# Eight row blocks of one expert moved from the expert stage to the end of a graph network's second layer

## The chip, the core and the metric

The kernel runs on one core of one Trainium2 chip. The metric is the device time of one execution in microseconds (us). The core has five engines that run their own instruction streams and meet through semaphores: PE (matrix multiply, with PEld for its weight loads), DVE (vector), ACT (scalar), POOL (GpSimd) and SP (which here only starts transfers). Transfers are started by SP, ACT and POOL and carried by 16 DMA engines.

## What is computed

A two-layer graph convolution over 3125 nodes with 256 features and 50000 edges, followed by a mixture of 16 experts in which each node uses its two best. The part after the first layer norm, cut to what matters here:

```python
for W, b, g, be in ((W1, b1, ln_g1, ln_b1), (W2, b2, ln_g2, ln_b2)):
    h_res = h
    h = _gcn_conv(h, row, col, ew, dis, W, b)
    h = jax.nn.relu(_layernorm(h, g, be)) + h_res
x = x + h
...
xn = _layernorm(x, axis=-1)
gate_logits = xn @ gate_w + gate_b
topk_vals, topk_idx = jax.lax.top_k(gate_logits, 2)
topk_w = jax.nn.softmax(topk_vals, axis=-1)
h = jax.nn.relu(jnp.einsum('bsh,ehf->bsef', xn, w1) + b1)
expert_out = jnp.einsum('bsef,efh->bseh', h, w2) + b2
y = xn + sum over the two choices of topk_w * expert_out
x = x + _layernorm(y) * gamma + beta
```

## The kernel before

`program` runs three stages in turn, each a block of five engine streams: `gnn` (both graph layers and the choice of experts), `experts` (the expert networks) and `combine` (the weighted sum, the last layer norm and the output). All engines meet at a barrier between two stages.

**The graph layers.** Nodes stand in 25 tiles of 128. A layer is a product of a weighted adjacency with a table of the transformed nodes: PE sums 25 matmuls for each of 26 groups of cells (L1373), which the code calls a turn; DVE and ACT split the sum into three bf16 parts (`take_rest`, `take_low`, L818 and L824), PE folds them onto node tiles (`combine(k)`, L1265), and DVE with ACT finishes a tile (`finish_tile`, L829 to L866): bias, layer norm, relu, residual, and in layer two also the norm that the experts read. Layer two works from the last tile to the first; `r` counts its tiles, so r = 24 is the last finished.

**The choice of experts**, in layer two, two turns behind the tile: PE turns the normalised rows (`turn_x2`, L1306) and multiplies by the gate (`gate`, L1314), DVE takes the two best experts (`choose`, L873 to L891), PE counts how many nodes chose each expert before (`count`, L1321), and DVE computes each node's slot in its expert's region (`seat`, L897 to L902). POOL keeps the residual (`keep_x1`, L566) and scatters node numbers and target rows to the slots in DRAM (L577, two transfers per tile), here called the homes.

**The experts.** Rows are worked in blocks of 128 slots of one expert. For a block, SP loads the 128 node numbers and targets (`load_ids`, L1512), POOL gathers the rows (`fetch`, L1468), PE turns them (`turn_x`, L1542), ACT copies them out of PSUM (L1634), PE multiplies by w1 (`up`, L1559), DVE adds b1 and applies relu (`relu_h`, L1709), PE multiplies by w2 (`down`, L1571), DVE adds row and b2 (L1719, L1724), and POOL scatters the 128 results (`send`, L1474). PE's stream is written as up of block b+1, turn of block b+2, down of block b. The first `FIXED` = 4 blocks are the first blocks of experts 0 to 3; the rest come from a table that DVE computes behind the barrier (L1680 to L1699, from the counts of all nodes), with a copy of the block's w1 by ACT into `w1s` (L1628). 58 blocks are worked always, and up to 6 more only where a register says that the table has more (`more`).

**The weights.** w1 and w2 of all experts lie in the memory that the graph layers use before. SP loads them as that memory comes free: most of w2 between the turns, w1 behind the last turns (L149, L154), and the four last halves (`UPS_LATE`, `DOWNS_LATE`) in the expert stage after ten loads of node numbers.

```python
for b in range(IDS_FIRST):
    load_ids(b)
for e in UPS_LATE:
    load_up(sp, e)
for e in DOWNS_LATE:
    load_down(sp, e)
```

## Time and profile before

| what | value |
|---|---|
| median of 3 runs | 1191.6 us (1189.5 to 1194.8) |
| the profiled execution: its own time | 1186.33 us |
| its span, first to last instruction | 1184.6 us |
| mean granted clock of PE | 0.976 of full speed |
| busy in the span: PE, DVE, ACT, POOL | 91%, 60%, 33%, 51% |
| row blocks worked in the expert stage | 58 |

The page gives busy shares over the whole span, and a row of the span in 40 slices for each engine, the granted clock of PE (PEclk) and the transfers. Shares over the span hide the places where PE stands still, so the stage between the second layer and the steady part of the expert stage is read from the timelines, instruction by instruction, and from windows cut at its borders.

### The profile page before, as it was taken

To read this page: it belongs to the slowest core of one execution; us is meant where nothing else is said; L and a number is where in the kernel's file an instruction comes from. 1 tells how busy PE (TensorE), PEld (TensorE's weight loads), DVE (VectorE), ACT (ScalarE), POOL (GpSimd) and SP (SyncE) were. 2 spreads that over 40 slices of the span, in tenths; PEclk is the share of its full clock that TensorE was granted. 3 is DMA by queue.
4 is the path that set the end of the run, shared out by engine and by line. 5 is a ranking of instruction groups with operands and counts; after the bars stand their busy time and mean duration, and the time that the engine had idled before them with its cause. 6 is when DMAs were issued, how large, how long until landed. Compare 5 with 4: busy or idle time off the path is not lost. (4 is left out here: it accounts for less than half of the span.)

```text
span 1184.6 us, 19696 instructions
## 1 busy us (share of the span) xinstructions
PE 1074.9 (91%) x6393; PEld 932.6 (79%) x6396; DVE 716.2 (60%) x2173; ACT 395.2 (33%) x908; POOL 605.6 (51%) x659
## 2 busy tenths in 40 slices
PE   3787889999999999799998999999991999999966
PEld 2666768888888888688787788888871899999965
DVE  8999990144454444234477777777776455555537
ACT  4758675212222222112222122222221233333347
POOL 6777777777777777760012121121123455555526
PEclk9999999999999999899999999999995999999989
DMA  6999920334333413131365345445436522222237
GB/s 239 312 392 378 373 114 2 118 112 144 135 112 127 152 57 112 56 112 56 128 241 187 129 163 182 160 149 193 165 125 210 179 72 70 71 73 73 72 94 264
DMA packets 80164, 180.80 MB, mean 153 GB/s; under 512 B 29042, under 2 KB 58364, under 8 KB 74044
## 3 DMA queue, kind: packets, MB, share of 16 engines
q1 hardware_dynamic: 48792, 151.67, 35.4%
q0 software_dynamic: 19776, 15.76, 4.9%
q10 hardware_dynamic: 11492, 12.07, 3.1%
q8 instruction: 54, 0.88, 0.3%
q14 instruction: 50, 0.41, 0.1%
HBM read 122.12 MB, written 57.33 MB: 151 GB/s over the span
## 5 line engine op out<-in xcount | busy, mean ns | idle before, releaser
L507 POOL DMA_INDIRECT weights_by_cell<-w_cell,cell x391 | 390.4, 999 | 131.6 <-issue 121.7
L1373 PE MATMUL ps<-x_rows,w 128*128 128x256 f32 x1250 | 283.5, 381 | 8.0 <-DMA w<-weights_by_cell 8.0
L1373 PE MATMUL ps<-w 128*128 128x256 f32 x1164 | 267.9, 382 | 0.0
L1373 PEld LDWEIGHTS ps<-x_rows,w 128*128 128x128 f32 x1250 | 234.7, 191 | 39.2 <-DMA w<-weights_by_cell 8.8
L1373 PEld LDWEIGHTS ps<-w 128*128 128x128 f32 x1164 | 213.9, 190 | 25.5
L566 POOL TENSOR_TENSOR x_rows<-hot,beta_b 128x256 f32<-128x256 f32 x25 | 18.1, 724 | 287.6 <-DVE hot L857 287.6
L1709 DVE TENSOR_SCALAR hidt<-ps,b1t 128x128 f32<-128x128 f32 x232 | 66.0, 344 | 89.3 <-PE ps L1559 88.5
L1559 PEld LDWEIGHTS ps<-xt,w1s 128*128 128x128 f32 x880 | 106.8, 192 | 5.0 <-ACT w1s L1628 2.2
L1571 PE MATMUL ps<-w,hidt 128*128 (+1 forms) x464 | 109.8, 379 | 0.0
L1559 PE MATMUL ps<-xt,w1s 128*128 128x128 f32 x880 | 107.2, 275 | 1.8 <-ACT xt L1634 1.8
L1474 POOL DMA_INDIRECT expert_rows_by_token<-yb,ids x58 | 57.5, 992 | 92.9 <-DVE yb L1724 92.5
L1571 PEld LDWEIGHTS ps<-w,hidt 128*128 128x128 f32 x464 | 83.6, 190 | 9.0
L1123 PE MATMUL ps<-key_part,pick 128*128 128x256 f16 x196 | 59.2, 408 | 33.1 <-DVE layer L714 32.4
L818 DVE TENSOR_TENSOR layer<-ps,layer 128x256 f32<-128x256 f32 x52 | 22.1, 426 | 86.1 <-ACT layer L1035 85.3
L1468 POOL DMA_INDIRECT xb<-normalised_rows,ids x60 | 59.0, 983 | 26.6 <-PE ps L1542 16.3
L1634 ACT ACTIVATE xt<-ps 128x256 f32<-128x256 f32 x60 | 23.0, 384 | 140.6 <-PE ps L1542 140.6
L1265 PE MATMUL ps<-layer 128*128 128x256 bf16 x444 | 56.9, 272 | 9.1 <-issue 7.1
L1159 PE MATMUL ps<-w,hot 128*128 128x75 bf16 x400 | 64.6, 319 | 0.0
L1628 ACT ACTIVATE w1s<-w 128x1024 f32 x56 | 59.2, 1057 | 7.5 <-DMA w<-in_L_ffn_w_dram 5.3
L1265 PEld LDWEIGHTS ps<-layer 128*128 128x128 bf16 x444 | 41.8, 98 | 24.8 <-issue 16.9
L577 POOL DMA_INDIRECT token_and_home_of_slot<-pair,slot_id x50 | 50.2, 1005 | 14.2 <-issue 11.3
L838 DVE COPY_PREDICATED layer<-mark,zeros 128x256 f32<-128x256 int32 x50 | 22.5, 450 | 55.3 <-ACT mark L1043 54.5
(250 smaller groups left out, 1554.8 us busy)
## 6 DMA issues: line engine op xcount, KB each, us to landing
w<-weights_by_cell SPq DMA_DIRECT2D x46, 1600.0 KB, 6.9
weights_by_cell<-w SPq DMA_DIRECT2D x26, 1600.0 KB, 8.7
w<-in_L_ffn_w_dram SPq DMA_DIRECT2D x32, 512.0 KB, 9.3
weights_by_cell<-w_cell,cell POOLq DMA_INDIRECT x391
w<-in_x_dram ACTq DMA_DIRECT2D x1, 3072.0 KB
hot<-in_x_dram ACTq DMA_DIRECT2D x24, 128.0 KB, 7.6
normalised_rows<-hot ACTq DMA_DIRECT2D x24, 128.0 KB, 6.5
out_dram<-w SPq DMA_DIRECT2D x24, 128.0 KB
```

What stands on the lines that cost most here:

```text
L507: pool.indirect_dma_start(adj[:, :], bass.IndirectOffsetOnAxis(ap=cell[0:m, c:c + 1].bitcast(U32), axis=0), w_cell[0:m, n, half * CH + j:h ...
L577: pool.indirect_dma_start(home[:, :], bass.IndirectOffsetOnAxis(ap=slot_id[0:m, k, d:d + 1].bitcast(U32), axis=0), pair[0:m, k, d, :], Non ...
L1123: mm = pe.matmul(bank(at, k * SBE, (k + 1) * SBE), pick[:, j:j + 1].to_broadcast([P, P]), key_part[:, g, :], start=True, stop=True)
L1159: mm = pe.matmul(bank(6, 0, 3 * NT), hot[:, i % DRING, :, k], hot_w[:, i % DRING, :, :, k].rearrange("p a b -> p (a b)"), start=(i == 0 an ...
L1265: mm = pe.matmul(bank(2 + i % 3, 0, D), fold_bits[:, k % 2, cols], ov_parts[:, k % 2, c, :], start=begins and c == 0, stop=ends and c == P ...
L1373: mm = pe.matmul(ov_bank(k), ring[:, place_of(k), s * P:(s + 1) * P], tab[q][:, s, :], start=(s == 0), stop=(s == NT - 1))
L1468: pool.indirect_dma_start(xb[:, b % ring, :], None, x2_dram[0:N, :], bass.IndirectOffsetOnAxis(ap=ids[:, b % IDS, 0:1].bitcast(U32), axis= ...
L1474: pool.indirect_dma_start(planes[:, :], bass.IndirectOffsetOnAxis(ap=ids[:, b % IDS, 1:2].bitcast(U32), axis=0), yb[:, b % 2, :], None).th ...
L1559: mm = pe.matmul(ph[s][:, f * P:(f + 1) * P], w, xt[:, s, c, :], start=(c == 0), stop=(c == KD - 1))
L1571: mm = pe.matmul(py[s], hidt[:, s, c, :], w, start=(c == 0), stop=(c == KF - 1))
L1628: act.activation(w1s[:, k, :, :].rearrange("p c f -> p (c f)"), w1[:, bass.ds(e * (KD * F), KD * F)], ACT.Copy).then_inc(w1_ready, 1)
L1709: ins = dve.tensor_scalar(hidt[:, s, c, :], ph[s][:, c * P:(c + 1) * P], bias, 0.0, ALU.add, ALU.max)
```

## The change

Before layer two ends, the counts over its first 19 tiles (r = 0 to 18) give the expert most chosen so far; experts 5, 6 and 12 are excluded, because their w2 comes late. Up to eight full blocks of that expert are known by then. `popular` on DVE picks it and writes the eight block places, SP loads its w1, b1 and b2 into buffers of their own (`w1e`, `b1e`, `b2e`), POOL gathers the rows, and the blocks are worked by PE, ACT and POOL: blocks 0 to 3 inside `gnn` between the last instructions of layer two (the down of block 3 behind the barrier), blocks 4 to 7 at the head of `experts`. For blocks 0 to 5 ACT does the relu and takes the output from PSUM, and POOL adds row and bias; from block 6 (`BY_ACT`) on DVE does both as before. The later stage works 50 blocks always (`RARE` is 14), the table leaves out what was taken (`taken`), and the four last weight halves are loaded before the barrier. Several buffers are shared or moved to make room (`key_part`, `cell`, `w_cell`, `mark`, `vec`, `wmat`, `own_diag`, `over`).

```diff
-IDS = 12
+EARLY, EARLY_IN, BY_ACT, EARLY_T = 8, 4, 6, 19
+IDS = 8
-RARE = 6
+RARE = 6 + EARLY
+GATE_AT = 6
...
+        def early_fetch(pool, j):
+            if j >= RING:
+                pool.wait_ge(x_turned, j - RING + 1)
+                pool.wait_ge(y_ready, j - RING + 1)
+            pool.wait_ge(ids_in[j % IDS], 16 * (j // IDS + 1))
+            pool.indirect_dma_start(
+                xb[:, j % RING, :], None, x2_dram[0:EARLY_T * P, :],
...
+        def early_bias(pool, j):
+            pool.wait_ge(x_turned, j + 1)
+            pool.wait_ge(xb_in[j % RING], 16 * (j // RING + 1))
+            pool.tensor_tensor(xb[:, j % RING, :], xb[:, j % RING, :], b2e, ALU.add).then_inc(x_biased, 1)
+
+        def early_add(pool, j):
+            pool.wait_ge(y_taken, j + 1)
+            pool.wait_ge(x_biased, j + 1)
+            pool.tensor_tensor(yb[:, j % 2, :], yb[:, j % 2, :], xb[:, j % RING, :], ALU.add).then_inc(y_ready, 1)
...
+        def early_relu(act, j, ph):
+            act.wait_ge(h_ps, j + 1)
+            if j >= 2:
+                act.wait_ge(out_ps, j - 1)
+            for c in range(KF):
+                ins = act.activation(hidt[:, j % 2, c, :], ph[:, c * P:(c + 1) * P], ACT.Relu, bias=b1e[:, c:c + 1])
+            ins.then_inc(hidt_ready, 1)
```

In `gnn`, SP's stream behind the last load of layer two:

```diff
+                for k in range(EXPERTS // WGROUP):
+                    sp.wait_ge(w_in[k], 16 * sum(e // WGROUP == k for e in DOWNS_IN_LAYER))
+                sp.sem_inc(early_w, 1)
+                sp.wait_ge(early_ready, 1)
+                sp.wait_ge(tab_ready[1], NT)
...
+                sp.wait_ge(homes_first, 32 * EARLY_T)
+                for j in range(EARLY):
...
+                    sp.dma_start(ids[:, j % IDS, :], home[bass.ds(at * P, P), :]).then_inc(ids_in[j % IDS], 16)
+                    if j == 2:
+                        sp.dma_start(b1e[:, :], eb1[bass.ds(expert, 1), :].rearrange("a (c p) -> p (a c)", p=P),
+                                     allow_slow_non_contiguous=True).then_inc(early_w, 16)
+                        sp.dma_start(b2e, eb2[bass.ds(expert, 1), :].to_broadcast([P, D])).then_inc(early_w, 16)
                 sp.wait_ge(ov_ps, 2 * VT - 2)
                 for e in (3, 4):
                     load_up(sp, e)
...
                 for e in UPS_IN_TIME:
                     load_up(sp, e)
+                sp.wait_ge(fold_ready, 2 * VT)
+                load_down(sp, DOWN_LATE)
+                sp.wait_ge(agg_read, 2 * NT)
+                load_up(sp, UP_LAST)
+                sp.wait_ge(z_ready, 2 * NT)
+                for e in DOWNS_LAST:
+                    load_down(sp, e)
```

In `gnn`, DVE in `seat`, then ACT:

```diff
+                    if r == EARLY_T:
+                        popular()
+                    if r == EARLY_T + 1:
+                        take_popular()
...
                 def marks(q, d, i):
+                    last = i == 2 * NT - 1
+                    if last:
+                        early_xt(act, 1, early_px)
+                        act.wait_ge(early_w, 49)
+                        early_relu(act, 0, bank(2))
                     act.wait_ge(y_made, i + 1)
...
+                    if last:
+                        early_relu(act, 1, bank(1))
                     act.wait_ge(z_made, i + 1)
...
+                    if last:
+                        early_y(act, 0, early_py)
+                        early_xt(act, 2, early_px)
```

In `gnn`, PE behind the last turn:

```diff
+                pe.wait_ge(early_w, 49)
...
+                turn_rows(pe, 0, early_px)
                 turn_x2(NT - 2)
+                pe.wait_ge(xt_ready, 1)
+                turn_rows(pe, 1, early_px)
+                pe.wait_ge(agg_read, 2 * NT - 1)
+                early_up(pe, 0, bank(2))
                 combine(2 * VT - 1)
                 gate(NT - 2)
                 count(NT - 3)
+                early_up(pe, 1, bank(1))
+                early_down(pe, 0, early_py, place)
+                turn_rows(pe, 2, early_px)
+                early_up(pe, 2, bank(2))
+                early_down(pe, 1, early_py, place)
                 turn_x2(NT - 1)
+                turn_rows(pe, 3, early_px)
                 gate(NT - 1)
                 count(NT - 2)
+                pe.wait_ge(agg_read, 2 * NT)
+                early_up(pe, 3, bank(3))
                 count(NT - 1)
...
+                early_down(pe, 2, early_py, place)
```

In `experts`, POOL's stream behind the barrier:

```diff
+                    fetch(6)
+                    finish_early(2)
+                    fetch(7)
+                    early_bias(pool, 4)
+                    finish_early(3)
+                    early_bias(pool, 5)
                     for k in range(XRING):
                         pool.wait_ge(x2_out[k], 16 * -(-(NT - k) // XRING))
...
+                    fetch(8)
+                    finish_early(4)
+                    fetch(9)
+                    finish_early(5)
+                    fetch(10)
```

`early_xt`, `early_up`, `early_down`, `early_y`, `turn_rows` and `send_rows` do for an early block what `copy_x`, `up`, `down`, the output addition, `turn_x` and `send` do for a later one; `popular` is a chain of small operations on 16 or 8 values, shown as rows below.

How the order of instructions moves, at three places. **PE, from the last turn's end to the barrier.** Before, only the turn of the last tile's rows (L1306), its gate (L1314), the counts (L1321, L1322) and the fold (L1265) stand there:

```order
L1306 MATMUL ps<-ident,hot 128x128 x2
L1265 MATMUL ps<-layer 128x256 x3
L1314 MATMUL ps<-gwt,ht 128x16 x2
L1321 MATMUL ps<-both,below 128x16
L1322 MATMUL ps<-before,ones 128x16
```

After, the same instructions (now L1521, L1480, L1529, L1538, L1539) have early work between them; a piece from the down of block 0 (its last weights) on:

```order
L231 MATMUL ps<-ident,xb 128x128 x2
L238 MATMUL ps<-xt_e,w1e 128x128 x8
L249 MATMUL ps<-w,hidt 128x256 x4
L1521 MATMUL ps<-ident,hot 128x128 x2
L231 MATMUL ps<-ident,xb 128x128 x2
L1529 MATMUL ps<-gwt,ht 128x16 x2
L1538 MATMUL ps<-both,below 128x16
L1539 MATMUL ps<-before,ones 128x16
L238 MATMUL ps<-xt_e,w1e 128x128 x8
```

L231 is the turn of an early block, L238 its up, L249 its down: the up of block 2 and the down of block 1 now stand ahead of the turn of the last tile's rows.

**POOL, the last homes.** Before, the last residual and the homes of the last three tiles (L577, two each) stand directly ahead of the barrier:

```order
L566 TENSOR_TENSOR x_rows<-hot,beta_b 128x256
L577 DMA token_and_home_of_slot<-pair,slot_id 59392x2 x6
L357 UNCONDITIONAL_BRANCH
L1453 UNCONDITIONAL_BRANCH
L1455 IOTA bnum 128x60
```

After (L716 the residual, L723 the homes, L195 and L200 the early additions, L204 an early block's results):

```order
L188 DMA xb<-normalised_rows,ids 128x256 x3
L195 TENSOR_TENSOR xb<-xb,zeros 128x256 x2
L723 DMA token_and_home_of_slot<-pair,slot_id 60416x2 x2
L200 TENSOR_TENSOR yb<-yb,xb 128x256
L204 DMA expert_rows_by_token<-yb,ids 66816x256
L716 TENSOR_TENSOR x_rows<-hot,beta_b 128x256
L195 TENSOR_TENSOR xb<-xb,zeros 128x256
L200 TENSOR_TENSOR yb<-yb,xb 128x256
L204 DMA expert_rows_by_token<-yb,ids 66816x256
L723 DMA token_and_home_of_slot<-pair,slot_id 60416x2 x4
L195 TENSOR_TENSOR xb<-xb,zeros 128x256
```

The homes of the last two tiles now stand behind the addition and the sending of early block 1.

**DVE, in `finish_tile` of tile r = 21**, ahead of the seat of tile 19 (L1096), new:

```order
L1068 TENSOR_TENSOR early_score<-ps,may_early 128x16
L1069 MAX early_top<-early_score 128x8
L1070 TENSOR_SCALAR fixed_one<-eids 128x16
L1071 MAX_INDEX early_at<-early_top,early_score 128x8
L1072 TENSOR_SCALAR early_f<-early_at 128x1
L1073 CAST early_e<-early_f 128x1
L1074 TENSOR_SCALAR early_place<-early_f 128x1
L1075 TENSOR_SCALAR early_lead<-early_f 128x1
L1076 SCALAR_TENSOR_TENSOR early_rows<-early_lead,early_top 128x1
L1077 TENSOR_SCALAR early_has<-rows_to,early_rows 128x8
L1078 SCALAR_TENSOR_TENSOR early_e<-early_f,early_place 128x1
L1079 TENSOR_REDUCE early_n<-early_has 128x1
```

Three more of the kind follow, and two in the next tile (`take_popular`); nothing is taken out of DVE's stream there.

## Rows read from the trace of the kernel before

**Rows 1.** Windows: stretch, busy us (count) PE PEld DVE ACT POOL, PEclk, DMA share, GB/s.

```profile
800.00:885.40 85.40, 85.11 (x451) 72.88 (x449) 66.13 (x222) 18.50 (x47) 16.80 (x19) 1.00 0.47 160
885.40:888.80 3.40, 0.59 (x5) 0.35 (x5) 2.66 (x12) 1.19 (x4) 2.00 (x3) 1.00 0.56 193
888.80:918.00 29.20, 4.68 (x25) 3.35 (x24) 18.97 (x68) 4.10 (x9) 10.79 (x14) 0.50 0.63 208
918.00:924.00 6.00, 6.00 (x34) 6.00 (x33) 1.13 (x4) 0.38 (x1) 1.93 (x2) 0.57 0.76 250
936.00:1139.00 203.00, 203.00 (x1420) 191.86 (x1419) 103.25 (x328) 78.12 (x109) 104.42 (x106) 1.00 0.23 70
```

**Rows 2.** PE's timeline, end of layer two to the first blocks: start, us.

```profile
884.82 0.59 PE L1373 MATMUL ps<-w 128*128 128x256 f32 x2
...
888.66 0.52 PE L1265 MATMUL ps<-layer 128*128 128x256 bf16 x3 [1.89 <-DVE layer L824]
...
897.49 0.69 PE L1306 MATMUL ps<-ident,hot 128*128 128x128 f32 x2 [7.59 <-DVE hot L866]
...
903.92 0.20 PE L1385 MATMUL ps<-before,ones 128*128 128x16 bf16 x1 [0.99 <-DVE slot_id L902]
...
918.10 6.13 PE L1559 MATMUL ps<-xt,w 128*128 128x128 f32 x32
924.07 0.38 PE L1542 MATMUL ps<-ident,xb 128*128 128x128 f32 x2
924.29 1.89 PE L1571 MATMUL ps<-w,hidt 128*128 128x256 f32 x8
```

**Rows 3.** PE's timeline, the steady part and the last block's down.

```profile
935.47 2.02 PE L1559 MATMUL ps<-xt,w1s 128*128 128x128 f32 x16 [1.82 <-ACT xt L1634]
...
943.01 1.95 PE L1559 MATMUL ps<-xt,w1s 128*128 128x128 f32 x16
944.79 0.38 PE L1542 MATMUL ps<-ident,xb 128*128 128x128 f32 x2
945.01 1.89 PE L1571 MATMUL ps<-w,hidt 128*128 x8
...
1139.06 1.89 PE L1571 MATMUL ps<-w,hidt 128*128 x8
```

**Rows 4.** SP's timeline in the expert stage: node numbers, then the late weight halves.

```profile
909.05 10.40 SPq L1512 DMA_DIRECT2D ids<-token_and_home_of_slot  x10
919.50 0.51 SPq L149 DMA_DIRECT2D w<-in_L_ffn_w_dram  x1
920.06 3.56 SPq L154 DMA_DIRECT2D w<-in_L_ffn_w_dram  x3
```

**Rows 5.** DVE's timeline: one turn's chain, then the last tile's seat.

```profile
876.03 0.42 DVE L824 TENSOR_TENSOR layer<-layer 128x256 bf16<-128x256 f32 x1 [0.26 <-ACT layer L1037]
...
888.09 0.42 DVE L824 TENSOR_TENSOR layer<-layer 128x256 bf16<-128x256 f32 x1 [0.26 <-ACT layer L1037]
...
900.18 0.17 DVE L897 TENSOR_TENSOR rank<-ps,base 128x16 f32<-128x16 f32 x1 [1.14 <-PE ps L1322]
...
901.03 0.17 DVE L873 TENSOR_TENSOR logit<-ps,gbias 128x16 f32<-128x16 f32 x1
...
903.69 0.17 DVE L902 CAST slot_id<-which 128x2 int32<-128x2 f32 x1
...
904.87 0.19 DVE L1678 TENSOR_TENSOR gap<-best 128x25 f32<-128x25 f32 x1
```

**Rows 6.** POOL's timeline: last residual, last home, first gather.

```profile
895.86 0.72 POOL L566 TENSOR_TENSOR x_rows<-hot,beta_b 128x256 f32<-128x256 f32 x1 [8.00 <-DVE hot L857]
...
905.42 0.97 POOL L577 DMA_INDIRECT token_and_home_of_slot<-pair,slot_id  x1 [0.30 <-issue]
...
911.59 1.00 POOL L1468 DMA_INDIRECT xb<-normalised_rows,ids  x1 [4.84 <-DMA ids<-token_and_home_of_slot]
```

**Rows 7.** Issues from 904 to 925: KB each, median us from issue to landing.

```profile
w<-in_L_ffn_w_dram SPq DMA_DIRECT2D x4, 512.0 KB, 10.2
...
xb<-normalised_rows,ids POOLq DMA_INDIRECT x6, 5.0
```

**Rows 8.** POOL's groups by shape: count | busy us, mean ns | idle before.

```profile
L566 POOL TENSOR_TENSOR x_rows<-hot,beta_b 128x256 f32<-128x256 f32 x25 | 18.1, 724 | 287.6 <-DVE hot L857 287.6
L1837 POOL TENSOR_TENSOR w<-w,x_rows 128x256 f32<-128x256 f32 x25 | 18.0, 726 | 19.9 <-ACT w L1831 18.4
```

**Rows 9.** Issues from 885 to 905, as in rows 7.

```profile
w<-in_L_ffn_w_dram SPq DMA_DIRECT2D x10, 512.0 KB, 9.5
...
token_and_home_of_slot<-pair,slot_id POOLq DMA_INDIRECT x7, 5.5
b1r<-in_L_ffn_b_dram ACTq DMA_DIRECT2D x1, 24.0 KB, 2.3
```

More of the change, by code:

```diff
@@ new lines, in early_y, with turn_rows @@
+        def early_y(act, j, py):
+            act.wait_ge(out_ps, j + 1)
+            if j >= 2:
+                act.wait_ge(y_out[j % 2], 16 * (j // 2))
+            act.activation(yb[:, j % 2, :], py, ACT.Copy).then_inc(y_taken, 1)
+        def turn_rows(pe, j, px):
+            pe.wait_ge(xb_in[j % RING], 16 * (j // RING + 1))
+            for c in range(KD):
+                mm = pe.transpose(px[:, c * P:(c + 1) * P], xb[:, j % RING, c * P:(c + 1) * P], ident[:, :])
+            mm.then_inc(x_turned, 1)
@@ L1320, in count @@
                         pe.wait_ge(rank_read, r)
+                    if r == EARLY_T:
+                        pe.matmul(bank(5, EXPERTS, 2 * EXPERTS), ones[:, :], before[:, r % 2, :], start=True, stop=True)
                     pe.matmul(bank(5, 0, EXPERTS), below[:, :], both[:, r % 2, :], start=True, stop=False)
@@ L1603, in _ @@
                     with pe.If(more(pe, "pe")):
[L1604 to L1605 removed]
+                        for b in range(USUAL, ALL):
+                            block_of_rows(b)
                 def load_b2(act, lo, hi, landed):
```

499 lines of the change are left out of this document (331 added, 168 removed).

## The prediction

> **What bounds the kernel now.** I read the page's slices first, then windows cut at the borders of the stages, then the timelines of PE, DVE, POOL and SP between the second layer and the steady expert stage. The windows [rows 1] show PE full in both neighbours: 85.1 of 85.4 us in layer two's last turns, and all of the 203 us from 936 to 1139. Between 885.4 and 918 it works 5.3 of 32.6 us, and from 888.8 on at half the granted clock (0.50, the 1.2 GHz level; 1.00 elsewhere). So the gap between two PE-bound stages is what early work can fill. What ends it is a chain of other engines [rows 2, 5, 6]: last sum at 885.4, last tile finished by DVE (its rows turned at 897.5), two more rounds of gate, choice and count, last seat at 903.9, last home issued from 905.4 to 906.4, node numbers fetched from 909.05 [rows 4], first gather at 911.6 [rows 6], first up at 918.1, and the even rhythm from the down at 924.29 on [rows 2].
>
> That rhythm sets the price of a block. The first down starts at 924.29, the 58th and last at 1139.06 [rows 2, 3]: 57 periods in 214.77 us, less one stall. The stall is the 1.82 us ahead of the up at 935.47 [rows 3]; it is put down to ACT's copy, which itself waited for the last four weight halves, issued from 919.50 to 923.62 [rows 4] and 10.2 us in landing [rows 7]. (214.77 - 1.82) / 57 = **3.736 us a block**.
>
> **What is removed.** The stage behind the even rhythm's start has eight blocks fewer: 8 x 3.736 = **29.9 us**. The four weight halves now go out behind the other ten before the barrier, some 20 us earlier, and land before the first wait for all weights; the stall goes: **1.8 us**. Nothing takes its place there, since ACT's copies of w1 then run two blocks ahead. Together 31.7 us; this is spent again, in part, in three places.
>
> **1. DVE's chain through layer two.** `popular` has 15 instructions and `take_popular` 2, all on 16 values or fewer. Four such linked ones take 901.03 - 900.18 = 0.85 us [rows 5], 0.21 each: 17 give 3.6. Five of them have nothing waiting for their result directly, which brings it down to some 2.9. I take **3.4**. Is there cover? One turn's DVE chain runs from L824 at 876.03 to L824 at 888.09 [rows 5]: 12.06 us, and the fold of the last turn on PE waits for it (1.89 us, DVE L824, rows 2), after the sums have ended. So the loop DVE, fold, DVE is what ends layer two; what is added to it arrives at its end in full.
>
> **2. PE, ACT and POOL inside the last tile.** ACT and PE work in order, so each early instruction stands in front of something. Walked with the durations of the rows: up 0 ends some 0.7 us after the last fold could start. Up 2 and down 1 stand ahead of the turn of the last tile's rows, which DVE waits for: up 2 waits for ACT's copy of the turned rows, this for the output of block 0, and both end about 2 us after the rows are ready. The relus by ACT, four of at most 0.4 us, fall into its waits for DVE (4.1 us of work in 29.2, rows 1). The first delay is partly taken up by DVE's wait for PE's next count (1.14 us at 900.18, rows 5). I take **1.8**, between 0 (all in the gaps) and 4.5 (both delays plus one more hand-over). POOL then has, between the last-but-two homes and the last, an addition, a sending and another residual: 23 us of work from the residual of tile 23 on, done at about the time when the last seat comes, so it adds nothing more; what is behind it, if it were late, is SP's wait for the homes.
>
> Of the DMAs, each engine issues its own: eight node number loads, w1, b1, b2 by SP (at 857 to 867, when SP waits for sums), six gathers by POOL before the barrier. They land long before PE asks, at about 889. The weights on SP's queue are 14 halves in a row instead of ten (9.5 us each in landing, rows 9); the last sends and homes share the DMA engines with them.
>
> **3. Behind the barrier.** Before: 924.3 - 904.8 = 19.5 us to the first steady down (DVE's first instruction there is at 904.87, rows 5). After: six ups, seven turns and five downs stand before the same point, at 1.78, 0.22 and 1.73 us [rows 3]: 20.9. ACT's two starts of transfers and its first copy stand ahead of the first up, 1.4, and the transpose of b1 is 0.4: 22.7. On POOL the gather of block 8 stands behind two gathers, two sends (1.3 each with the gap), four additions (0.9 each with the gap) and three iotas: some 9.3, begun 2 us after the barrier, when POOL still issues homes; with 5.0 us to landing [rows 7] its rows are there 16.3 us after the barrier, where PE would want them after 14.8. PE waits 1.6: 24.3, that is **4.8** more than before. Ends: 2.5 (steady PE work alone, with the copies hidden) and 7.5 (both gathers 6 to 7 as the homes were, and DVE's table, begun at its iotas, later too). I take 4.8 because its three parts have rows at this place. The node numbers for block 8 come by then: homes 5.5 [rows 9] after an issue that ends 2 us behind the barrier, and 2 for the load, 9.5 against POOL's 11.3.
>
> By the Trainium skill, page "SBUF — State Buffer", section "Who interferes with whom", GpSimd and VectorE share a port pair: a vector instruction with two SBUF inputs contends with a GpSimd instruction that reads SBUF. POOL's 128x256 addition takes 724 ns beside layer two and 726 ns in the last stage [rows 8], so no row shows it stretched. By that rule up to four additions before the barrier would wait for a 0.43 us instruction each, 1.7 us by estimate, and the gain would be 20 instead of 21.7; I go by the rows.
>
> **Sum.** 31.7 - 3.4 - 1.8 - 4.8 = **21.7 us**. From the profiled execution's 1186.3 that is 1164.6. This execution lies 5.3 below the median of the three runs; from the median, 1191.6 - 21.7 = **1169.9**, stated as 1170. With all three losses at their good ends (2.9, 0, 2.5) it is 1165.3, with all at their bad ones (3.6, 4.5, 7.5) 1175.5.
>
> **The rivals.** *The clock stays at half.* PE fell to 0.50 from 888.8 to 918 with 16% of that stretch worked, and two ups then took 6.13 us at 0.57 where one takes 1.95 at 1.00 [rows 1 to 3], so 1.1 more for an up and, in proportion, 1.0 for a down. Ups 0 to 2 and downs 0 and 1 in part (some 3.5) and the first three pieces behind the barrier (3.2) would cost about 7: 1177. Against it: PE's gaps from 889 on are 1 to 3 us by my walk, and a 1.82 us gap at 933.6 left the clock at 1.00. By the Trainium skill, page "TensorE: Matmul & The Clock Gate", section "What's actually happening", the throttled state is the default and activity releases it; the trace agrees (0.57, then 1.00, once blocks run).
>
> *POOL or the transfers hold block 8.* If gathers land after 6 to 7 us and the sends of blocks 0 and 1 come as late, POOL's line of waits (an addition waits for ACT, ACT for the down, the next gather for the addition) grows by 5 to 9 us: 1175 to 1179. For it: POOL has no slack by my walk. Against: the rhythm of one gather and one send a block was kept from 936 on.
>
> *Slower: the early weights come late.* PE waits for w1e, b1e and b2e ahead of the turn of tile 23's rows, and all that ends layer two is queued behind that wait on PE. b1e is 512 single words; the nearest row is the b1 load of 24 KB, 2.3 us [rows 9], and no row shows such single words. Needed at about 889, they would cost a microsecond for each after that; the gain is gone when they land at 911, and at 925 the time is 1206. Against: SP can start them at 857.
>
> *It doesn't do what it says.* If the chosen expert had fewer than eight full blocks, spare blocks would be worked and the table would pass its limit of 46; 14 more blocks would follow (52 us): about 1222. The reference's routing for these inputs gives expert 2 with 1527 rows in the first 19 tiles, against 1152 needed, and 46 later blocks, exactly the limit; so this is nearly excluded.
>
> **Chances.** Forecast 0.63 (1163 to 1175), half clock 0.15, POOL or transfers 0.11, these two together, no more than 0.5% from no change, 0.05; weights late 0.05 and too few blocks 0.01, both slower. 0.5%, 6 us, is about what a measurement of this kernel can tell from no change. Faster 0.89, same 0.05, slower 0.06. The range, 1163 to 1181, takes in the bounds of the sum, the runs' spread of 2 to 3 us below and the two milder rivals; it leaves out some 0.15 to 0.2.
>
> **What would show it.** Right: 8 x 3.74 us fewer in the steady stage, no wait ahead of the first copied w1, the last fold on PE some 3 to 4 us later than 888.7, the last home 5 to 6 later than 905.4, the down of block 8 at about 934, and the granted clock at 1.00 through the gap. Wrong: the clock at 0.50 behind 889, PE waiting for block 6's, 7's or 8's rows by more than 2 us each, a wait of PE for w1e, or a rhythm other than 3.74.

## The result and the profile after

| | before | after | ratio, 95% interval |
|---|---|---|---|
| median of 4 runs each | 1192.18 us | 1177.24 us (1175.62 to 1182.97) | 0.9891 [0.9863, 0.9919] |
| the changed kernel run again: 6 runs, against 17 of before | 1190.81 us | 1177.90 us | 0.9896 [0.9878, 0.9915] |

The change is faster, by 14.9 us in the first comparison and 12.9 in the second. The forecast was 1170, a gain of 21.7, so 7 to 9 us of it are missing. The profiled execution took 1175.62 us with a span of 1173.9.

PE's timeline shows the core of the change as it was forecast. These are rows of the changed kernel from the last fold to the steady stage (start, us), answering to [rows 2, 3]:

```profile
896.31 0.49 PE L1480 MATMUL ps<-layer 128*128 128x256 bf16 x3
...
898.92 1.89 PE L249 MATMUL ps<-w,hidt 128*128 x8
900.64 0.38 PE L231 MATMUL ps<-ident,xb 128*128 128x128 f32 x2
903.58 2.94 PE L238 MATMUL ps<-xt_e,w1e 128*128 128x128 f32 x16 [2.55 <-ACT xt_e L212]
906.31 2.71 PE L249 MATMUL ps<-w,hidt 128*128 x8
908.85 0.38 PE L1521 MATMUL ps<-ident,hot 128*128 128x128 f32 x2
...
938.88 1.89 PE L1805 MATMUL ps<-w,hidt 128*128 128x256 f32 x8
...
948.07 1.95 PE L1792 MATMUL ps<-xt_e,w1s 128*128 128x128 f32 x16
...
1121.73 1.89 PE L1805 MATMUL ps<-w,hidt 128*128 x8
```

L238 and L249 are ups and downs of early blocks, L1521 is the turn of the last tile's rows. The first steady down, block 8's, starts at 938.88 and the last one at 1121.73: 49 periods of 3.732 us. The up on the first copied w1, at 948.07, has no wait ahead of it: the 1.82 us stall of [rows 3] is gone. Behind the barrier PE is nearly never idle, as the windows show (columns as in [rows 1]):

```profile
889.00:900.00 11.00, 10.30 (x72) 9.33 (x71) 8.56 (x32) 4.16 (x13) 6.24 (x7) 1.00 0.51 179
900.00:910.00 10.00, 7.14 (x36) 6.05 (x35) 6.80 (x20) 4.57 (x16) 6.89 (x9) 0.83 1.05 349
910.00:918.00 8.00, 5.63 (x40) 4.58 (x40) 4.93 (x22) 1.89 (x7) 6.33 (x11) 1.00 1.04 356
918.00:936.00 18.00, 17.99 (x124) 16.45 (x123) 14.29 (x31) 5.37 (x17) 15.08 (x17) 1.00 0.51 108
936.00:1121.70 185.70, 185.70 (x1297) 175.47 (x1296) 94.07 (x301) 71.07 (x99) 97.41 (x99) 1.00 0.27 80
```

Where PE worked 4.68 of 29.2 us at a granted clock of 0.50 [rows 1], it now works 23.07 of 29 at 1.00, but for the stretch from 900 to 910 (0.83). To see where the missing microseconds are, I cut every profile of this study at the same five instructions: A, from the start to DVE's statistics of tile 17 of layer two (still ahead of the changed region); B, from there to the rank of the last tile; C, from there to the first steady down; D, to the start of the last matmul of the last down; E, to the end of POOL's last addition; F, to the end of the span.

| us | A | B | C | D | E | F |
|---|---|---|---|---|---|---|
| before | 804.8 | 98.3 | 21.3 | 216.3 | 40.1 | 4.0 |
| after | 808.7 | 104.5 | 25.6 | 184.4 | 41.3 | 9.3 |
| e1_again (the changed kernel) | 809.9 | 103.3 | 25.3 | 184.4 | 41.6 | 9.3 |
| e2_pe_pad | 813.3 | 104.5 | 25.3 | 184.4 | 43.3 | 9.3 |
| e3_weights_only (of before) | 805.2 | 98.3 | 22.2 | 214.2 | 39.9 | 4.0 |
| e4_pick_twice | 813.0 | 107.4 | 26.3 | 184.4 | 44.0 | 9.3 |
| e5_no_drain | 808.1 | 104.4 | 26.3 | 184.4 | 42.1 | 4.6 |
| e6_pool_pad | 811.8 | 104.5 | 25.7 | 184.4 | 41.2 | 9.3 |
| e7_before_no_drain (of before) | 809.6 | 98.3 | 20.6 | 217.6 | 40.3 | 4.1 |
| e8_small_adds | 811.0 | 102.5 | 26.5 | 184.4 | 42.6 | 9.3 |
| e9_more_gathers | 807.9 | 104.4 | 25.4 | 184.4 | 47.7 | 4.5 |
| e10_act_order | 810.6 | 102.9 | 26.2 | 184.4 | 44.3 | 4.6 |
| e11_pick_beside | 812.8 | 100.1 | 25.3 | 184.4 | 41.5 | 4.6 |
| e12_before_gathers (of before) | 810.9 | 98.2 | 20.5 | 217.2 | 44.6 | 3.9 |

Three things stand out. A varies from profile to profile of one and the same program, mostly with PE's waits for the adjacency; from tile 0 of layer two to tile 17 all fourteen profiles take 214.1 or 214.2 us, so the spread lies ahead of layer two. So the difference of two spans says little here, and what an experiment does is read from its own stage. B is 103.3 in e1 and 104.4 to 104.5 in the other profiles of the changed kernel with the same code there; the section on the choice of the expert shows why. And F, a stage that the change doesn't touch, is 5.3 us longer in every profile of the changed kernel that keeps its closing barrier, except e9. SP's waits at the end, in the changed kernel:

```profile
SPq L2055 <- PEq L2055: 5.0, 1, 5.0
SPq L2055 <- DMA out_dram<-w: 3.8, 1, 3.8
```

and before:

```profile
SPq L1786 <- DMA out_dram<-w: 3.3, 1, 3.3
SPq L1786 <- PEq L1786: 0.2, 1, 0.2
```

After the last store has landed SP waits another 5.0 us in the closing barrier, where it waited 0.2.

### The profile page after: what moved, and what is told of

It reads as the page before. It is cut to its first block and busy times, and to the rows that moved or that the text cites. A ratio compares the mean times of both kernels' runs of the same rounds, so it can differ in the third digit from the quotient of the medians.

```text
span 1173.9 us, 19637 instructions
## 1 busy us (share of the span) xinstructions
PE 1076.2 (92%) x6397; PEld 932.1 (79%) x6397; DVE 713.3 (61%) x2156; ACT 395.7 (34%) x930; POOL 617.2 (53%) x676
## 5 line engine op out<-in xcount | busy, mean ns | idle before, releaser
L650 POOL DMA_INDIRECT weights_by_cell<-hidt x391 | 392.0, 1003 | 132.5 <-issue 123.0
L1590 PEld LDWEIGHTS ps<-w 128*128 128x128 f32 x1164 | 214.6, 191 | 25.7
L716 POOL TENSOR_TENSOR x_rows<-hot,beta_b 128x256 f32<-128x256 f32 x25 | 18.1, 723 | 279.3 <-DVE hot L1030 279.3
L204 POOL DMA_INDIRECT expert_rows_by_token<-yb,ids x58 | 57.6, 994 | 78.0 <-DVE yb L1990 75.5
L1967 DVE TENSOR_SCALAR hidt<-ps,b1t 128x128 f32<-128x128 f32 x200 | 56.3, 344 | 67.4 <-PE ps L1792 67.4
L1805 PE MATMUL ps<-w,hidt 128*128 (+1 forms) x400 | 94.6, 379 | 0.0
L1792 PEld LDWEIGHTS ps<-xt_e,w1s 128*128 128x128 f32 x752 | 91.4, 192 | 2.4
L1792 PE MATMUL ps<-xt_e,w1s 128*128 128x128 f32 x752 | 91.5, 275 | 0.0
L1338 PE MATMUL ps<-xt_e,pick 128*128 128x256 f16 x196 | 58.9, 406 | 34.7 <-DVE layer L887 34.2
L1805 PEld LDWEIGHTS ps<-w,hidt 128*128 128x128 f32 x400 | 72.1, 190 | 7.7
L1480 PE MATMUL ps<-layer 128*128 128x256 bf16 x444 | 57.6, 274 | 8.3 <-issue 8.2
L1480 PEld LDWEIGHTS ps<-layer 128*128 128x128 bf16 x444 | 42.0, 98 | 24.1 <-issue 15.9
L1880 ACT ACTIVATE xt_e<-ps 128x256 f32<-128x256 f32 x52 | 20.0, 384 | 117.1 <-PE ps L231 117.1
L723 POOL DMA_INDIRECT token_and_home_of_slot<-pair,slot_id x50 | 50.2, 1004 | 11.9 <-issue 11.1
L1011 DVE COPY_PREDICATED layer<-mark_a,zeros 128x256 f32<-128x256 int32 x50 | 22.5, 450 | 55.7 <-ACT mark_a L1251 54.9
L1338 PEld LDWEIGHTS ps<-xt_e,pick 128*128 128x128 f16 x196 | 16.5, 117 | 49.0 <-DVE layer L887 39.0
```

Of the source, the lines that this page charges most:

```text
L204: pool.indirect_dma_start(planes[:, :], bass.IndirectOffsetOnAxis(ap=ids[:, j % IDS, 1:2].bitcast(U32), axis=0), yb[:, j % 2, :], None).th ...
L650: pool.indirect_dma_start(adj[:, :], bass.IndirectOffsetOnAxis(ap=cell[0:m, c:c + 1].bitcast(U32), axis=0), w_cell[0:m, n, half * CH + j:h ...
L723: pool.indirect_dma_start(home[:, :], bass.IndirectOffsetOnAxis(ap=slot_id[0:m, k, d:d + 1].bitcast(U32), axis=0), pair[0:m, k, d, :], Non ...
L1011: link(dve.copy_predicated(y, mark_a[:, 0:D].bitcast(I32), zeros[:, 0:D]))
L1338: mm = pe.matmul(bank(at, k * SBE, (k + 1) * SBE), pick[:, j:j + 1].to_broadcast([P, P]), key_part[:, g, :], start=True, stop=True)
L1480: mm = pe.matmul(bank(2 + i % 3, 0, D), fold_bits[:, k % 2, cols], ov_parts[:, k % 2, c, :], start=begins and c == 0, stop=ends and c == P ...
```

## The experiments

### The changed kernel again, and PE's code moved

e1_again is the changed kernel without an edit. e2_pe_pad puts waits on PE ahead of the last stage:

```diff
         def _(pe):
+            for k in range(128):
+                pe.wait_ge(diag_ready, 1)
             for t in range(NT):
```

> The changed kernel as it is, with a second profiled execution. In the first, 7 of the 21.7 us that were forecast are missing, and the trace shows differences outside the changed region: +3.9 us in the graph stage (1.4 in the first 15 us, 2.2 at a wait for the adjacency at 496) and 5.0 us at the very end, where SP waits for PE's queue after the last store has landed. Theory (the end belongs to the new program, the graph stage is chance): the 5.0 us at the end come again, within 0.5; the +3.9 us do not, the second profile has them at 0 to 2; median 1177, plus or minus 2. Rival (all of it chance, the terms of the gap were too small): the wait at the end is under 1 us here, and the losses between the two layers and block 8 come out above 11 us.

> The changed kernel with 128 waits on a semaphore that is long set, put on PE ahead of its first product of the last stage, where PE waits 9 us for the first rows anyway. It changes nothing but the place of PE's later instructions in its code. Theory (PE's queue is late at the end since its last instructions fall behind a border of its code that has to be loaded): the 5.0 us wait of SP for PE's queue at the end is under 1 us, the time 4 to 5 us under the changed kernel, about 1172.5. Rival (something else holds PE's queue there, such as the length of the program or the last products): the wait stays at 5.0 us and the time at 1177.

e1_again: 1177.90 us; the wait at the end is 5.0 us again, so it is the program's own. A is 809.9, 5.1 above the first profile of before: the +3.9 did not go away, against my theory. But three more profiles of programs that are the old one up to there (e3, e7, e12) have 805.2, 809.6 and 810.9, and the ten of the changed program lie between 807.9 and 813.3. The means are 3 us apart, the spread within either is as large: whether the change costs something in the graph stage stays open.

e2_pe_pad: ratio 0.9919 [0.9900, 0.9938], 1181.48 us, and the wait is 5.0 us as before. The 128 waits were not free: the first product of the last stage comes 13.8 us behind the end of the last down instead of 9.2. The theory on PE's code has fallen all the same, since the wait did not move. The name in that row misled me: all engines count up one semaphore in the barrier, and the row names one that does so. The rows of the barrier's line itself (its instructions by engine: duration in ns, min/median/max, first and last start) name the late one. Of the changed kernel:

```profile
L2055 PEldq DRAIN  x1: 957/957/957, 1160.1 to 1160.1; - x1
...
L2055 POOLq DRAIN  x1: 10411/10411/10411, 1163.2 to 1163.2; - x1
```

and of the one before:

```profile
L1786 POOLq DRAIN  x1: 2732/2732/2732, 1179.3 to 1179.3; - x1
```

PE's queue had ended its own DRAIN there at 1161. POOL's DRAIN lasts until 1163.2 + 10.4 = 1173.6, and the span ends at 1173.9.

### The closing DRAIN

e5_no_drain leaves POOL's DRAIN out of that barrier, e7_before_no_drain does so in the kernel before; SP still waits for all stores:

```diff
-    with nc.Block() as block:
+    with nc.Block(no_gpsimd_drain=True) as block:
```

e6_pool_pad puts 64 waits on POOL, as e2 did on PE:

```diff
         def _(pool):
+            for k in range(64):
+                pool.wait_ge(diag_ready, 1)
             for t in range(NT):
```

> The changed kernel, with POOL's DRAIN in the closing barrier of the last stage left out; SP's wait for the landing of all stores stays. In every profile of the changed program so far POOL's DRAIN there takes 10.41 us, in those of the program before 2.73, and SP waits 5.0 and 0.2 us after the stores have landed. Theory (the DRAIN is what SP waits for, the name PE in that row is only the engine that arrived at the same semaphore): 5.0 us less, 1172.9 against 1177.9, and the span ends 0.3 us after the last store has landed. Rival (PE's queue is late on its own): 1177.9 and the wait of 5.0 us stays.

> The changed kernel with 64 waits on a long-set semaphore on POOL ahead of its first addition of the last stage, where POOL has 18 us of idle time. Theory (the DRAIN is long since the instruction behind it lies across a border of POOL's code and has to be loaded): the DRAIN falls from 10.4 to some 3 us, the time by 5 to 1173. Rival (it is the work that POOL itself has to close, the same in each run): DRAIN 10.4 and 1178 again.

> The kernel before with the same DRAIN left out. Theory: there it is hidden behind the landing of the stores but for 0.2 us, so the time stays at 1190.8, within 1. Rival: it delays more than the trace shows, 1188 or less.

e5: 1172.10 us against 1192.42 of before in the same comparison, ratio 0.9835 [0.9813, 0.9858]. F falls from 9.3 to 4.6 us, and SP's rows of that kernel read as they did before the change:

```profile
SPq L2055 <- DMA out_dram<-w: 3.8, 1, 3.8
SPq L2055 <- PEq L2055: 0.2, 1, 0.2
```

So the DRAIN is what held the end, and it cost some 5 us of the gain. With it gone the gain is 20.3 us by medians. e7: ratio 0.9995 [0.9982, 1.0009]: in the program before, the DRAIN was hidden behind the stores. e6: 0.9894 [0.9871, 0.9917], and DRAIN again 10.41 us: moving POOL's code by 64 waits does not change it.

What makes it long? e9 adds four gathers to the changed kernel, behind POOL's last send:

```diff
+                    for k in range(4):
+                        pool.indirect_dma_start(
+                            xb[:, k, :], None, x2_dram[0:NT * P, :],
+                            bass.IndirectOffsetOnAxis(ap=ids[:, 0, 0:1].bitcast(U32), axis=0)).then_inc(y_out[0], 16)
+                    pool.wait_ge(y_out[0], 16 * (USUAL // 2) + 64)
                     pool.wait_ge(table_ready, 1)
```

> The changed kernel with four more gathers of 128 rows by POOL, behind its last send and awaited there, in the idle time ahead of the last stage; DRAIN kept. All that is asked is the length of POOL's DRAIN, 10.41 us in five profiles of the changed program, 2.73 in two of the one before, 64 more waits without effect. Theory (it depends on how many indirect transfers POOL has issued, or on what is left of them in its queue): another length than 10.41, by 0.2 us or more. Rival (it depends on something else in the program): 10.41 again. The time is for neither, a few us above 1178.

```profile
L2060 POOLq DRAIN  x1: 2897/2897/2897, 1168.5 to 1168.5; - x1
```

e9: 1176.04 us in one run, with E 6 us longer, since the last stage starts behind the four gathers, and DRAIN 2.90 us. So the four transfers change the DRAIN, where 64 more waits did not. e12_before_gathers adds the same four to the kernel before:

```diff
+                    for k in range(4):
+                        pool.indirect_dma_start(
+                            xb[:, k, :], None, x2_dram[0:N, :],
...
+                    pool.wait_ge(y_out[0], 16 * (usual // 2) + 64)
```

> The kernel before with the same four more gathers by POOL behind its last send, DRAIN kept. In the changed kernel they brought POOL's DRAIN from 10.41 to 2.90 us. Theory (the length goes up and down with how many indirect transfers POOL has issued, 559 in both programs without the four): another length than 2.73 here, possibly the long one. Rival (the short DRAIN is what such gathers leave behind, or what the program before has anyway): 2.7 to 2.9 again.

There the DRAIN goes from 2.73 to 3.06 us (one run, 1197.08 us). In both programs the length moves when POOL issues more, but the number of transfers does not set it: both programs issue 559 indirect ones, with 2.73 us in the one and 10.41 in the other. What does set it stays open.

### The late weights alone

e3_weights_only moves only SP's last four loads in the kernel before:

```diff
+                sp.wait_ge(fold_ready, 2 * VT)
+                load_down(sp, 12)
+                sp.wait_ge(agg_read, 2 * NT)
+                load_up(sp, 5)
+                sp.wait_ge(z_ready, 2 * NT)
+                for e in (5, 6):
+                    load_down(sp, e)
...
-                    for e in UPS_LATE:
-                        load_up(sp, e)
-                    for e in DOWNS_LATE:
-                        load_down(sp, e)
```

> The kernel before with only the last four weight halves moved: they go out behind the other ten in the graph stage. Theory (the prediction's second term): PE's 1.82 us wait ahead of the first copied weights is gone and nothing takes its place: 1192.2 - 1.8 = 1190.4, no block saved. Rival: the halves now share the DMA engines with the last homes and the first gathers, the first up comes later by as much as was won: 1192, and the gap to the down at 924.3 is longer by 1 to 2 us.

Ratio 0.9999 [0.9986, 1.0011]. D is 2.1 us shorter, so the stall is gone; C is 0.9 longer than in the profile of before. PE's timeline of e3 shows both:

```profile
910.61 0.37 PE L1537 MATMUL ps<-ident,b1r 64*128 64x64 f32 x1 [6.14 <-DMA b1r<-in_L_ffn_b_dram]
...
925.58 1.89 PE L1574 MATMUL ps<-w,hidt 128*128 128x256 f32 x8
...
934.78 1.95 PE L1562 MATMUL ps<-xt,w1s 128*128 128x128 f32 x16
```

No wait stands at 934.78, but b1, which [rows 9] has landing in 2.3 us, is waited for here for 6.14 us, while it was 4.8 before. Theory and rival are both right in part, and the time can't tell them: by itself this edit buys at most 1.7 us (the lower end of the interval). The stall and the start of the blocks go together: in the two later profiles of the old code, e7 and e12, the stall is 3.09 and 2.73 us instead of 1.82, and C is 0.7 and 0.8 shorter, so that C and D together are 237.6, 238.2 and 237.7 us in the three, and 236.4 in e3. D also gives the cleanest price of the blocks: 214.2 - 184.4 = 29.8 us for eight, both without the stall.

### The choice of the expert

e4_pick_twice runs the 15 instructions of the choice two times:

```diff
                     if r == EARLY_T:
+                        popular(False)
                         popular()
```

> The changed kernel with the 15 instructions that choose the expert done twice, one pass after the other, at the same place on DVE. Theory (the loop of DVE and PE has no slack in layer two, so the chain arrives in full at the end): 2.4 us more by the traced length of the chain to 3.1 by the prediction's 0.21 us an instruction: 1179.6 to 1180.3. Rival 1 (it is partly covered, the loss seen there is a short drop of PE's clock): under 1 us more. Rival 2 (the longer pause drops PE's clock for longer): over 4 us more.

Ratio 0.9933 [0.9910, 0.9956], 1182.92 us, 5.0 over e1. By the time alone rival 2 would have it (over 4), but both intervals reach 2 us or more to either side, and A and E, which the edit doesn't touch, are 3.1 and 2.4 longer in its profile than in e1's. B is 107.4, 2.9 to 4.1 us over the two profiles of the changed kernel. To tell chain and clock apart I cut B at DVE's statistics of single tiles (tile 17 to 20 takes 38.0 us in every profile):

| us | tile 20 to 21 | 21 to 23 | 23 to 24 | 24 to the last rank | granted clock, 21 to 22 |
|---|---|---|---|---|---|
| before | 12.7 | 24.9 | 11.2 | 11.6 | 1.00 |
| after | 15.1 | 26.2 | 11.2 | 14.1 | 0.87 |
| e1_again | 15.1 | 25.0 | 11.2 | 14.1 | 1.00 |
| e4_pick_twice | 17.6 | 26.5 | 11.1 | 14.1 | 0.75 |
| e8_small_adds | 15.1 | 26.2 | 11.1 | 12.1 | 0.87 |
| e10_act_order | 15.1 | 26.2 | 11.1 | 12.5 | 0.88 |
| e11_pick_beside | 12.7 | 25.2 | 11.2 | 13.1 | 1.00 |

The choice stands in the first of these stretches: it costs 2.4 us there, and the second pass of e4 2.5 more. So the chain arrives in full, and the theory holds for it. The second stretch shows the drop of PE's clock that the rivals speak of: 1.3 us more behind the choice in the first profile, 0.1 in e1. PE waits equally long in both, ahead of the turn (0.67 us) and of the fold, and runs the fold at two speeds (the first row is of the first profile, the second of e1):

```profile
870.08 1.80 PE L1480 MATMUL ps<-layer 128*128 128x256 bf16 x9 [1.41 <-issue]
...
871.25 1.14 PE L1480 MATMUL ps<-layer 128*128 128x256 bf16 x9 [1.41 <-issue]
```

The granted clock is 0.66 from 870 to 875 in the first profile and 1.00 from 871 to 876 in e1. e2, e5, e6 and e9 are like the first (26.0 to 26.2 us, 0.87 to 0.88). So PE pauses for the choice, and where the clock falls behind that pause it costs up to 1.3 us more; in e4 the clock is 0.50 from 875 to 880, and the stretch is 1.6 longer than before the change. So the rivals are right that the clock takes part, but with the smaller share.

e11_pick_beside (which also has e10's order and no DRAIN) takes these 17 instructions out of their row: a list hands one out behind each of the main chain's instructions.

```diff
+                def beside():
+                    if side:
+                        make, linked = side.pop(0)
+                        if side_at[0]:
+                            dve.wait_ge(v, side_at[0])
+                        ins = make()
...
                 def link(ins):
-                    dve.wait_ge(v, did(ins))
+                    at = did(ins)
+                    beside()
+                    dve.wait_ge(v, at)
```

> The kernel with ACT's order changed and without the DRAIN, and the 17 instructions that choose and note the expert no longer in a row: each is issued behind one of the main chain's instructions, ahead of that one's wait. Theory (term 1 is latency, not work): 2.5 to 3 us of the 3.4 come back, the last seat at 99.5 to 100.5 behind the start of tile 17, the time 2.5 to 3 us under the one without it, about 1167.5; the early weights are then asked for some 10 us later and still land before PE wants them at about 890. Rival 1 (they cost the same anywhere on DVE): no gain. Rival 2 (the weights now come too late): PE waits ahead of the turn of tile 23's rows, the gain is lost.

1170.07 us, ratio 0.9814 [0.9787, 0.9842]; B is 100.1, 2.9 below e10. By the table the 2.4 us of the choice are gone, and 1.1 behind it, since the clock stays at 1.00 there; 0.6 is lost from tile 24 on, where up 3 runs at 0.81 granted (909 to 917). DVE's timeline of e11 shows why (L1089 to L1092 belong to the choice, the others to the main chain):

```profile
862.36 0.19 DVE L1119 TENSOR_TENSOR picked<-one,rank 128x32 f32<-128x32 f32 x1
862.47 0.17 DVE L1089 TENSOR_TENSOR early_score<-ps,may_early 128x16 f32<-128x16 f32 x1
862.58 0.19 DVE L1121 TENSOR_REDUCE which<-picked 128x2 f32<-128x32 f32 x1
862.68 0.17 DVE L1090 MAX8 early_top<-early_score 128x8 f32<-128x16 f32 x1
```

The main chain goes from 862.36 to 862.58 with an instruction of the choice in between, 0.22 us, as far as it goes without one (860.65 to 860.88 in the changed kernel). The early weights are asked for 6.5 us later (873.4 instead of 862.8, less the 4.1 by which A differs), and PE still doesn't wait for them.

### The last tile: POOL's additions and ACT's order

In the changed kernel some of DVE's instructions of the last tile are long (DVE's timeline):

```profile
899.80 0.84 DVE L1015 SCALAR_TENSOR_TENSOR layer<-layer,small,vec 128x256 f32<-128x256 f32 x1
...
903.49 1.25 DVE L1030 TENSOR_TENSOR hot<-layer,hot 128x256 f32<-128x256 f32 x1
...
910.53 0.17 DVE L1096 TENSOR_TENSOR rank<-ps,base 128x16 f32<-128x16 f32 x1 [2.28 <-PE ps L1539]
```

Both overlap additions of POOL. These are little longer than the 0.72 us of [rows 8]: 0.74 and 0.96 in the pair of the first row, 0.73 in the second:

```profile
899.58 1.64 POOL L195 TENSOR_TENSOR xb<-xb,zeros 128x256 f32<-128x256 f32 x2
...
903.71 0.73 POOL L200 TENSOR_TENSOR yb<-yb,xb 128x256 f32<-128x256 f32 x1
```

e8_small_adds cuts the additions ahead of the barrier to one column:

```diff
-            pool.tensor_tensor(xb[:, j % RING, :], xb[:, j % RING, :], b2e, ALU.add).then_inc(x_biased, 1)
+            n = 1 if j < 4 else D
+            pool.tensor_tensor(xb[:, j % RING, 0:n], xb[:, j % RING, 0:n], b2e[:, 0:n], ALU.add).then_inc(x_biased, 1)
...
-            pool.tensor_tensor(yb[:, j % 2, :], yb[:, j % 2, :], xb[:, j % RING, :], ALU.add).then_inc(y_ready, 1)
+            n = 1 if j < 2 else D
+            pool.tensor_tensor(yb[:, j % 2, 0:n], yb[:, j % 2, 0:n], xb[:, j % RING, 0:n], ALU.add).then_inc(y_ready, 1)
```

> The changed kernel with POOL's six additions that stand ahead of the barrier (four of b2, two of x) done on one column instead of 256: blocks 0 to 3 lack b2 and blocks 0 and 1 lack x in 255 of 256 columns. Theory 1 (VectorE's instructions with two inputs wait for POOL's additions): the product with the gain in the last tile, 1.25 us in the changed kernel and 0.42 elsewhere, and its neighbours (0.84, 0.63, 0.65) are back at 0.4 to 0.5, the last seat comes 1.5 to 2 us earlier behind the start of tile 17 of layer two (105 to 103), and the time falls by as much, to 1176. Theory 2 (the stretched ones lie beside waits for PE and ACT, which are what counts): those instructions are short again, but the last seat moves by less than 0.5 us.

DVE's timeline of e8, the same two instructions:

```profile
902.07 0.49 DVE L1017 SCALAR_TENSOR_TENSOR layer<-layer,small,vec 128x256 f32<-128x256 f32 x1
...
905.26 0.43 DVE L1032 TENSOR_TENSOR hot<-layer,hot 128x256 f32<-128x256 f32 x1
```

They are back at 0.49 and 0.43, and B is 102.5 instead of 104.5 in the first profile; the 2.0 us lie between tile 24 and the last rank (12.1 instead of 14.1): theory 1 holds in its stage. The time does not show it: the ratio, 0.9892 [0.9870, 0.9915] (1179.51 us, not 1176), is that of the changed kernel. C is 0.9 longer here, with a wait of 0.99 us by PE for gathered rows, and the rest is less than A and E vary.

e10_act_order (without DRAIN) moves two instructions of ACT:

```diff
                     if last:
                         early_relu(act, 1, bank(1))
+                        early_y(act, 0, early_py)
+                        early_xt(act, 2, early_px)
                     act.wait_ge(z_made, i + 1)
...
-                    if last:
-                        early_y(act, 0, early_py)
-                        early_xt(act, 2, early_px)
```

> The changed kernel without the closing DRAIN, and with ACT's two early instructions of the last tile (the copy of block 0's output and of block 2's turned rows) moved ahead of ACT's wait for that tile's sum, instead of behind it. Theory (PE waits 2.55 us for that copy, so block 2's up and block 1's down run late, at half clock, and hold up the turn of the last tile's rows by 2.2 us): up 2 starts 1.5 us earlier, the turn comes right behind the last normalisation, the last seat 1.5 to 2 us earlier behind the start of tile 17 of layer two (104.4 without the move), the steady stage by as much, 1170.3 against 1172.1 for the one without DRAIN. Rival (DVE's chain sets it, stretched by POOL's additions): the last seat moves by less than 0.5 us.

PE's timeline of e10:

```profile
903.64 2.05 PE L238 MATMUL ps<-xt_e,w1e 128*128 128x128 f32 x16 [0.70 <-ACT xt_e L212]
905.53 1.89 PE L249 MATMUL ps<-w,hidt 128*128 x8
908.80 0.44 PE L1520 MATMUL ps<-ident,hot 128*128 128x128 f32 x2 [1.38 <-DVE hot L1039]
```

PE waits 0.70 instead of 2.55 us for the copy, up 2 and down 1 take 2.05 and 1.89 instead of 2.94 and 2.71, and the turn of the last tile now waits for DVE, where DVE's rows had waited for PE. B is 102.9, and from tile 24 to the last rank it takes 12.5 instead of 14.1: 1.6 less. In the time it is not to be seen: 0.9842 [0.9816, 0.9869] against e5's 0.9835 [0.9813, 0.9858], with A 2.5 and E 2.3 us longer in its profile than in e5's.

e11 beats the kernel before and the changed one: 1.9% under the kernel before, and its interval [0.9787, 0.9842] lies below that of the changed kernel [0.9878, 0.9915]. Against e5 and e10 its gain is shown in B alone; the intervals of the times overlap.

## Why the prediction was right or wrong

**The side and the order of size were right**: faster, 1177 inside the range, but a gain of 13 to 15 instead of 21.7.

**What is removed: right.** 29.8 us for eight blocks were measured where 29.9 stood, rhythm 3.732 against 3.736. The stall was worth 2.1 in D against the first profile (it is longer in e7 and e12); nothing took its place, since b1 is turned behind block 5 in the changed kernel, where its later landing, seen in e3, holds nobody.

**1. DVE's chain: the mechanism right, the number by luck.** 3.4 was forecast. The 15 instructions cost 2.4 and the second pass of them 2.5; the 2 of the next tile cost at most 0.1 (25.0 against 24.9 in e1). The walk at 0.21 us an instruction was 1 us too long. What fills it up to 3.4 in the mean is PE's clock behind the pause, 1.2 to 1.3 us in five profiles of six and 0.1 in e1, which the term does not contain. Putting all 17 beside the chain gave the 2.4 back: they are latency and no work, which the walk didn't say.

**2. The last tile: one cause right, one put at nothing.** 1.8 us was to come from PE and ACT working in order, and nothing from POOL. B grew by 6.0 (the mean is 104.3 in the six profiles that have the changed code there, 98.3 in four with the old); 2.6 of that lies from tile 24 on (14.1 against 11.6). Taking out ACT's order gives back 1.6 of it (e10), taking out most of POOL's additions 2.0 (e8); the two overlap, and no run takes out both. The step that failed is the sentence "no row shows it stretched": [rows 8] are POOL's own additions, and I looked for the delay there. It is DVE that waits, 1.25 us for 0.42. By the Trainium skill, page "SBUF — State Buffer", section "Who interferes with whom", such a pair of instructions contends for a shared port, and which one blocks depends on the order of issue. e8 agrees that they contend, with 2.0 us where the estimate by that rule was 1.7; the rows don't bear out the order: DVE's product starts at 903.49 and POOL's addition at 903.71, and DVE's is the one stretched (starts on POOL are rough).

**3. Behind the barrier: PE's part right, the sum by luck.** 4.8 was forecast; C is 25.6 in the mean of the same six, 20.8 in the three of the old code with its late weights (before, e7, e12): 4.8. But C starts at the last rank, and 0.9 of the 4.8 lies ahead of the barrier: from the last rank to DVE's first instruction behind it 2.73 us pass, 1.83 before. Behind it the first steady down comes after 22.6 to 23.0 us in five of the six profiles, as the walk had it without POOL (22.7; PE works 17.99 of 18 us from 918 to 936). The 1.6 us for POOL's gather did not come as a wait of PE there; in e5 it is 0.56. And since C is short where the stall in D is long, the two are better taken together: 237.8 in the mean of those three before, 210.0 in that of the six after, 27.8 saved where 31.7 - 4.8 = 26.9 stood.

**The rivals.** The clock at half came in part, and at two places: 0.69 granted from 904.5 to 910 in the changed kernel, behind PE's wait of 2.55 us, which cost 0.99 on up 2 and 0.82 on down 1, and 0.66 from 870 to 875, ahead of the stretch that the rival looked at. POOL and the transfers did not hold block 8 in the first profile: no wait of PE is left between 918 and the last down. The gathers issued at 897.33 and 898.60 took 6.9 and 7.0 us to land, those at 921.13 and 926.69, behind the barrier, 3.2 and 2.8. In e4, e5, e8 and e10 PE waited 0.45 to 0.99 us for gathered rows there, so POOL's part is small but not nothing. The early weights were there: PE doesn't wait for them; its 0.70 us ahead of the turn of tile 23's rows are for DVE's rows. The blocks were full.

**What the sum lacked: the end.** F, 5.3 us, has no term in the prediction. I read the work of the last stage as untouched, which it is; but its closing barrier contains an instruction of POOL whose length changes with what POOL issued earlier, and I had moved POOL's transfers (that this move is what lengthened it was not tried by itself). In the profile of before this DRAIN was hidden (0.2 us), so no row of the waits pointed at it, but the rows of the barrier's line would have shown that it exists. E is 1.3 us longer in the first pair as well; what in the last stage's loads causes it was not tried.

The ledger of the first pair, unrounded: D gave 31.9 us; B took 6.2, C 4.4, E 1.3 and F 5.4. 31.9 - 17.3 = 14.6 are left, against 14.9 and 12.9 measured; the sum leaves A out. What A adds, 0 to 3 us, can't be told from its spread.

**What would show it.** The last fold came 3.7 us later by the change (896.31 against 888.66, less the 4.0 of A), block 8's down at 934.9 by the same count, both as said; but 1.3 of the 3.7 is the clock, and in e1, without it, the last fold is 2.5 later. The last home came 6.2 later, a little late; the clock's 1.00 through the gap failed between 900 and 910.

## What to carry to other kernels

Before work is moved, list what each engine does in the barriers behind it, not only what it computes: an instruction that was hidden there can come out, and it is read from the rows of the barrier's line, since a wait in a barrier may name the wrong engine. When an engine gets new work beside a critical chain, look for the delay in the chain's own instructions, not in the new ones. A chain of small linked instructions costs its latencies; handed out one by one behind those of another chain, it cost next to nothing here: the 2.4 us came back, and with them 1.1 us of PE's clock behind the pause. A pause that is put into one engine's chain can cost again on another, and whether it does can differ between two runs of one program; so look at the granted clock behind it in more than one profile.

## What was not expected of the hardware

POOL's DRAIN lasted 10.41 us in six profiles of the changed program, 2.73 in two of the one before, 2.90 and 3.06 with four more gathers, with all of POOL's transfers landed long before. DVE's additions with both inputs in SBUF took up to 1.25 us beside POOL's, whose own took 0.72 to 0.96. The clock is not settled by the length of PE's waits alone: in the changed kernel's first profile and in e1, one program with the same waits of 0.67 and 1.41 us, the fold behind them took 1.80 and 1.14 us, at 0.66 and 1.00 granted. In e10 up 3 took 2.02 us, behind waits of 0.70, 1.38, 0.26 and 0.21 us; in e11, with the first three alone, it took 3.31, at 0.81 granted from 909 to 917.
